# Block quantization scales on VectorE instead of ScalarE, and a second buffer for the quantized activations

## What is computed

```python
def block_quant(v, m_bits, bk):          # m_bits 3, bk 32
    vb = v.reshape(*lead, K // bk, bk)
    amax = jnp.max(jnp.abs(vb), axis=-1, keepdims=True)
    e = jnp.floor(jnp.log2(jnp.maximum(amax, 2.0 ** -126)))
    scale = jnp.exp2(e - m_bits)
    return jnp.round(vb / scale) * scale

h = einsum(block_quant(x), block_quant(w_fc)) + b_fc      # 1024 -> 4096
h = gelu(h)
y = einsum(block_quant(h), block_quant(w_proj)) + b_proj  # 4096 -> 1024
```

## Time and profile before

| | us |
|---|---|
| median of 2 runs (4010.78 to 4011.41) | 4011.1 |
| the profiled execution | 4003.8 |
| its span, slowest core (core 7) | 4002.3 |
| spans of the eight cores | 3974.5 to 4002.3 |
| mean granted TensorE clock, core 7 | 0.785 of full |

### The profile page before, as it was taken

How to read it: one execution, slowest core, us unless ns; L and a number is a source line. 1 busy time by engine, 2 the same in 40 slices (tenths; PEclk the granted TensorE clock), 3 DMA queues, 4 the chain that set the end, 5 groups by cost and what they waited for, 6 DMA issues and landing times.

```text
span 4002.3 us, 33325 instructions; the slowest of 8 cores (3974.5 to 4002.3 us)
## 1 busy us (share of the span) xinstructions
PE 1943.5 (49%) x10624; PEld 968.4 (24%) x10624; DVE 1372.1 (34%) x2279; ACT 1460.6 (36%) x3983; POOL 29.9 (1%) x60
## 2 busy tenths in 40 slices
PE   0111116666666666666666665246565333433333
PEld 0100012222222222222222222234343221211121
DVE  4555544434344344434434444311211112121111
ACT  2333335555555555555555554000000023321111
POOL 0000000000000000000000000000000100000000
PEclk9999998888888888888888888566858765655555
DMA  1222110000000000000000001420000310004443
GB/s 47 64 67 64 58 61 16 27 24 16 27 27 14 27 27 20 21 27 24 16 27 24 16 22 34 106 45 11 22 11 11 66 24 0 0 13 147 147 143 138
DMA packets 62579, 168.27 MB, mean 42 GB/s; under 512 B 9923, under 2 KB 10179, under 8 KB 62408
## 3 DMA queue, kind: packets, MB, share of 16 engines
q1 hardware_dynamic: 54344, 151.47, 11.2%
q0 software_dynamic: 8064, 14.68, 2.2%
HBM read 138.84 MB, written 41.94 MB: 45 GB/s over the span
## 4 chain that ended last, share of the span: by engine, by line
PE 33%; ACT 20%; DVE 17%; DMA 13%; DVEq 8%; issue 7%; SPq 2%; POOL 1%; ACTq 0%; POOLq 0%
PE psB L573 8%; DVEq L342 7%; PE psA L527 6%; ACT hqT_t L365 4%; DMA gp<-g_s 4%; PE psB L850 4%; PE psB L864 4%; ACT L545 3%; DMA wstg<-wproj 3%; DMA wstg<-wfc 3%; PE psB L356 3%; DVE ib L343 3%; ACT hb_t L545 3%; DVE hq_t L345 2%; DVE wqb L345 2%
## 5 line engine op out<-in xcount | busy, mean ns | idle before, releaser
L573 PE MATMUL psB<-WpjqT,hqT_t 128*128 128x512 bf16 x2048 | 568.9, 441 | 220.3 <-ACT hqT_t L365 167.6
L527 PE MATMUL psA<-WfcqT,xqT_t 128*128 128x512 bf16 x2048 | 495.5, 398 | 54.4 <-ACT xqT_t L365 54.4
L317 DVE TENSOR_REDUCE amx<-hb_t 128x32 f32<-128x1024 f32 x128 | 156.2, 1220 | 710.2 <-ACT hb_t L545 710.2
L573 PEld LDWEIGHTS psB<-WpjqT,hqT_t 128*128 128x128 bf16 x2048 | 216.1, 110 | 536.2 <-issue 386.2
L365 ACT CAST hqT_t<-psB 128x128 bf16<-128x128 f32 x1024 | 186.3, 306 | 389.7 <-PE psB L356 389.6
L356 PE MATMUL psB<-I128b_sb,wqb 128*128 128x128 bf16 x512 | 64.7, 306 | 506.3 <-DVE wqb L345 506.3
L527 PEld LDWEIGHTS psA<-WfcqT,xqT_t 128*128 128x128 bf16 x2048 | 200.8, 102 | 329.4 <-issue 128.4
L356 PE MATMUL psB<-I128b_sb,hq_t 128*128 128x128 bf16 x1024 | 95.6, 249 | 346.0 <-DVE hq_t L345 346.0
L324 ACT ACT_TABLE_LOAD x129 | 165.5, 1283 | 207.0 <-DVE amx L317 207.0
L854 ACT ACTIVATE Hbt<-psB 128x232 bf16<-128x232 f32 x128 | 46.5, 363 | 471.3 <-PE psB L850 471.3
L545 ACT ACT_TABLE_LOAD x128 | 164.2, 1283 | 100.9 <-PE psA L531 99.2
(11 more groups left out here) (122 smaller groups left out, 2579.6 us busy)
## 6 DMA issues: line engine op xcount, KB each, us to landing
wstg<-wfc SPq DMA_DIRECT2D x32, 512.0 KB, 3.5
wstg<-wproj SPq DMA_DIRECT2D x32, 512.0 KB, 3.6
xt<-x SPq DMA_DIRECT2D x32, 512.0 KB, 4.0
g_s<-g_t SPq DMA_DIRECT2D x32, 512.0 KB, 2.9
xnbp<-xnb_s SPq DMA_DIRECT2D x64, 256.0 KB, 2.6
xp<-x SPq DMA_DIRECT2D x32, 512.0 KB, 4.7
gp<-g_s SPq DMA_DIRECT2D x32, 512.0 KB, 5.2
out<-ob SPq DMA_DIRECT2D x32, 512.0 KB, 3.0
```

Source lines behind the costliest of these rows:

```text
L317: b.plain("vector", lambda e: e.tensor_reduce(qv["a"], qv["src3"], axis=AX.X, op=AluOpType.max, apply_absolute_value=True))
L527: st=(K == 0): e.matmul(o, l, r, start=st, stop=False))
L573: st=st: e.matmul(o, l, r, start=st, stop=False))
```

## The change

`q_scales` moves from ScalarE to VectorE. The maximum is clamped from below, its exponent bits are kept with a bitwise and (which gives the power of two itself), an eighth of that is the scale `sc`, and its reciprocal is `rs`. Each step is an instruction on 128x32 with a drain around it, and it follows the max-reduce directly in VectorE's queue. All three users of `q_scales` are changed: the weight units, the parts of the hidden activations, and the tile's input. `q_apply` waits for ScalarE no more. `hq_t` gets two slots, by the parity of w, and `v_apply(w)` waits for the transposes of part w-2.

```diff
--- before.py
+++ after.py
@@ -320,23 +320,21 @@
         qv["vA"] = b.seal("vector", "V")
 
     def q_scales(qv):
-        b.wait("scalar", "V", qv["vA"])
-        b.plain("scalar", lambda e: e.activation(qv["y"], qv["a"], AF.Ln))
-        b.seal("scalar", "S")
-        b.wait("scalar", "S")
-        b.plain("scalar", lambda e: e.activation(
-            qv["e32"], qv["y"], AF.Identity, scale=ccol("invln2"),
-            bias=ccol("mhalf")))
-        b.seal("scalar", "S")
-        b.wait("scalar", "S")
-        b.plain("scalar", lambda e: e.activation(
-            qv["rs"], qv["e32"], AF.Exp, scale=ccol("nln2"), bias=ccol("p3ln2")))
-        b.plain("scalar", lambda e: e.activation(
-            qv["sc"], qv["e32"], AF.Exp, scale=ccol("pln2"), bias=ccol("n3ln2")))
-        qv["sB"] = b.seal("scalar", "S")
+        b.plain("vector", lambda e: e.drain())
+        b.plain("vector", lambda e: e.tensor_scalar_max(qv["a"], qv["a"], 1e-37))
+        b.plain("vector", lambda e: e.drain())
+        b.plain("vector", lambda e: e.tensor_scalar(
+            qv["e32"], qv["a"].bitcast(I32), 0x7F800000, None,
+            op0=AluOpType.bitwise_and))
+        b.plain("vector", lambda e: e.drain())
+        b.plain("vector", lambda e: e.tensor_scalar_mul(
+            qv["sc"], qv["e32"].bitcast(F32), 0.125))
+        b.plain("vector", lambda e: e.drain())
+        b.plain("vector", lambda e: e.reciprocal(qv["rs"], qv["sc"]))
+        b.plain("vector", lambda e: e.drain())
+        qv["sB"] = None
 
     def q_apply(qv):
-        b.wait("vector", "S", qv["sB"])
         b.plain("vector", lambda e: e.tensor_tensor(
             qv["t3"], qv["src3"], qv["rs3"], op=AluOpType.mult))
         b.plain("vector", lambda e: e.drain())
@@ -427,7 +425,7 @@
     xq_t = sb("xq_t", (128, 2048), BF16, es01)
     xqT_t = sb("xqT_t", (128, 2048), BF16, es01)
     hb_t = sb("hb_t", (128, 2048), F32, es01)
-    hq_t = sb("hq_t", (128, 1024), BF16, es01)
+    hq_t = sb("hq_t", (128, 2048), BF16, es01)
     hqT_t = sb("hqT_t", (128, 1024), BF16, es01)
     g_t = sb("g_t", (128, 1024), F32, es01)
     lnst = sb("lnst", (128, 16), F32, es01)
@@ -547,12 +545,13 @@
 
         def mk_qh(w):
             hs = (w % 2) * 1024
-            return q_views(hb_t.ap()[:, hs:hs + 1024], 32, hq_t.ap(),
-                           32 + 32 * (w % 2), 0)
+            return q_views(hb_t.ap()[:, hs:hs + 1024], 32,
+                           hq_t.ap()[:, hs:hs + 1024], 32 + 32 * (w % 2), 0)
 
         def t_tr(w):
             b.wait("tensor", "V", chk[(i, w, "ap")])
-            chk[(i, w, "tr")] = t_transpose8(hq_t.ap())
+            chk[(i, w, "tr")] = t_transpose8(hq_t.ap()[:, (w % 2) * 1024:
+                                                       (w % 2) * 1024 + 1024])
 
         def s_te(w):
             chk[(i, w, "te")] = s_evac8(
@@ -584,8 +583,10 @@
             chk[(i, w, "am")] = qh["vA"]
 
         def v_apply(w, qh):
-            if (i, w - 1, "tr") in chk:
-                b.wait("vector", "T", chk[(i, w - 1, "tr")])
+            if (i, w - 2, "tr") in chk:
+                b.wait("vector", "T", chk[(i, w - 2, "tr")])
+            elif (i - 1, w + 2, "tr") in chk:
+                b.wait("vector", "T", chk[(i - 1, w + 2, "tr")])
             q_apply(qh)
             chk[(i, w, "ap")] = qh["done"]
```

## The result

The changed kernel takes 4065.3 us (median of 11 runs, 4050.2 to 4073.8), the kernel before 4011.5 in the same session; the ratio is 1.013, with a 95% interval of 1.011 to 1.015. The forecast was 4003, with a range up to 4050. So the kernel became slower by some 51 us (54 by the two medians) where 8 us less were forecast. Within 2% it is, but the sign and the range were wrong.

What follows compares the result with a forecast made beforehand. No engine near full; chains of waits bound each stage. Weight stage +84, waits -49, +1 and -25, clock -33 and +14 sum to -8 us, so 4011 - 8 = 4003 us, range 3950 to 4050.

Steps and rivals of the forecast that it cites:

- The chain s: New scale chain on VectorE, four small instructions with five drains between reduce and multiply: 1.34 us.
- the cheap end: Rival in the scale chain: reciprocal at 0.20 us, chain 1.13 us, 27 us less, 3976 us; chance 0.18.
- The weight stage: Load loop of the weight units: the new chain delays the next load in 63 of 64 units, +84 us.
- The three waits: TensorE's waits before transposes of w=0, w=2 and the next input: -49, +1 and -25 us.
- TensorE's clock: Token stage: slow first matmul groups go, -33 us; f(0) and f(2) stay slow for longer, +14 us.
- a microsecond taken out of one of them shortens the tile by as much: Token stage: chains ending at TensorE's three waits set a tile's length, so it follows them one to one.
- the slow first groups: First matmul group of a tile, 6.39 against 3.61 us, in 11 to 12 tiles; expected to go, -33 us.
- The charge for f(0) and f(2): Token-stage matmuls behind long waits: their slow start lasts longer after shorter waits, +14 us, bounds 0 and 37.
- the half microsecond: Sign of a wrong forecast: the clock at f(0) and f(2) moves by over half a microsecond a tile.
- The first term: TensorE's clock in the token stage: slow first groups go once the 0.80 us idle is gone, -33 us.
- the clock isn't won back: Rival: slow first groups stay, or f(0) and f(2) lose the gain; 4036, or 4059 us; chance 0.15.

Runs made afterwards that it cites:

- e7_token_fill_all: Kernel before with token-stage scales on VectorE, two hq slots, weight units on ScalarE, unused matmuls in every TensorE idle stretch of a tile: 3791.7 us, ratio 0.944.
- e9_before_fill_all: Kernel before plus unused matmuls in the token stage, 32, 14 and 3 in three waits, 6 behind each of five transposes: 3864.9 us, ratio 0.963.

## Why the prediction was wrong

**The chain s** was right: 1.37 in the weight stage and 1.44 in the token stage (from reduce to multiply 1157.22 to 1159.80, less 1.14) against 1.34. Within it the three plain steps were 0.18 (forecast 0.166), the drains 0.07 to 0.10 (0.07), and the reciprocal 0.353 (0.415), which is 6.2 ns per element from 2 to 32, (353 - 166)/30. That the sum is closer than its terms is luck: the reciprocal was taken too dear, the other steps and the drains too cheap. The repeat count of 8 in the Trainium skill (VectorE: DVE Perf Modes, "First, the fixed hardware budget") pointed the right way, off the cheap end. Taken as eight cycles per element, the forecast's 8.3 ns, it is a third too dear here.

**The weight stage** was right: +87 to +89 against +84.

**The three waits** were right, in size and place: -1.5, 0, -0.8 us a tile. That ScalarE would go from Gelu straight to the layernorm with one table load between them is seen in its rows in time, after:

```profile
1150.36 1.08 ACT L543 ACTIVATE hb_t<-psA 128x512 f32<-128x512 f32 x2
1151.33 1.15 ACT L454 ACTIVATE xn_t<-xt,lnst 128x1024 f32<-128x1024 f32 x1
...
1152.65 1.28 ACT L459 ACT_TABLE_LOAD   x1
...
1153.94 0.39 ACT L459 ACTIVATE lnst<-lnst,cst 128x1 f32<-128x1 f32 x1
...
1154.74 1.28 ACT L543 ACT_TABLE_LOAD   x1
```

From gelu(0) to the table load for gelu(1) 3.3 us pass, with a forecast of 3.39. Square still runs under Gelu's table and Ln brings its own. The Trainium skill (ScalarE: Activation LUTs, "What ACT_TABLE_LOAD costs") gives each load 1.38 us of drain beside the load; here Ln starts at 1153.94, when the load that began at 1152.65 has run its 1.28. From Square's end (1152.48) to Ln 1.46 us pass in all. By the rows no such drain exists at this place, as the forecast took it.

**TensorE's clock** is the step that failed, in both its terms, and with it the sentence that "a microsecond taken out of one of them shortens the tile by as much". "With the 0.80 gone I expect these to go: -33 us": the slow first groups became more, not fewer. Those of 6.4 us did go, and groups of 5.1 to 5.3 came in 26 of the 32 tiles. L525 stands 42 us over its full-clock time, where it was 31. In the settled tiles each first group takes 5.13 us. The granted clock of the changed kernel around such a start, in stretches of a microsecond:

```profile
2420.00:2421.00 1.00, 0.00 (x0) 0.00 (x0) 0.00 (x0) 1.00 (x7) 0.00 (x0) 0.99 0.00 0
2421.00:2422.00 1.00, 0.70 (x2) 0.28 (x3) 0.00 (x0) 0.98 (x2) 0.00 (x0) 0.50 0.00 0
...
2424.00:2425.00 1.00, 1.00 (x6) 0.38 (x4) 0.00 (x0) 0.00 (x0) 0.00 (x0) 0.80 0.60 250
```

TensorE worked from 2414.9 to 2419.6 without a break, at full clock, and idled for 1.69 us; at 2421 the clock is at 0.50 (1.2 GHz), and it comes back during 2424. The argument was that the same 1.69 before f(1) had left the clock high. One place in the tile was taken as the proof for another, and what TensorE had done before was not the same; which of the differences decides, no run shows. The rows of before spoke against the argument already: the fast first group at 1064.01 stood behind 1.97 us, more than the 1.69 of the slow one at 1002.17, and the 0.80 is there in fast and slow tiles alike (2307.23 and 2365.20, above). The charge for f(0) and f(2), "0.45 x 32 = +14 us", was too small as well: 26 us in the matmuls and 6 in the transposes ahead of them. Its upper bound of 37 would have held it. That is 0.8 us a tile in the matmuls, over the half microsecond that the forecast had named as a sign of being wrong. The first term was 44 us off (+11 for -33). The rival "the clock isn't won back" let the 33 go, and with the upper bound of the charge reached 4059, but never let the first groups lose on top; and the range stopped at 4050.

With the clock's part held near zero by fillers the rest of the sum is confirmed: +11 by weight stage and waits, +10 measured (+14 by the ratios). Why the clock gives back as much as it does, and why whole tiles settle on 58.0 us with different waits in them, stays open.

## What to carry to other kernels

Where TensorE idles in every iteration, a shorter wait need not be a shorter iteration: add up the engine's busy time for the same instructions before and after, beside its idle time, and give the clock's term both signs. To measure what a change of the waits is worth, hold the clock up in both versions; a half-filled wait does not do it. And where such waits can't be removed, unused matmuls in them may be worth more than the change itself: with the weight units' scales left on ScalarE (where nothing waited for them), the token stage's moved to VectorE, and the waits filled, the kernel takes 3792 us, 5.6% less than before, and by the two ratios (0.944/1.013) 6.8% less than the changed one.

## What the runs showed of the hardware

- Adding 70 matmuls of 512 columns to a tile (26, 14, and 6 at five places) takes it from some 58.1 to 52.1 us. All eight cores kept a granted clock of 1.00 over 22 tiles with TensorE busy for 94% of the time (e7_token_fill_all).
- Full clock is not certain with such filling: in the profiled execution of e9_before_fill_all two of the eight cores had a granted clock of 0.81 from 1880 to 2036 us, and 16 matmuls took 4.36 us. No run shows what brings it on.
- Tiles with different waits can have nearly one length: an ordinary tile before, one of the changed kernel and one without the clamp last 57.97, 58.02 and 58.02 us, with 11.7, 9.5 and 9.0 us of waits for VectorE in them.
- The clock fell at the end of an idle stretch as short as 1.69 us, after 4.7 us of unbroken work (changed kernel, 2421 us, above), and behind the one of the same length at 2414.9, just ahead of that work, it did not fall.
- A max-reduce and a multiply that follow each other directly overlap by 0.08 us; a drain between costs 0.07 to 0.10 us, so four small steps with five drains cost 1.37 us, of which 0.89 are the steps.
